# Two-layer transformer on one core: the row shift in two steps, the FFN's chunk stores regrouped, the absorbed weights stored from GpSimd's queue

## The chip, the cores and the metric

The kernel runs on one core of a Trainium2 chip. The metric is device time in microseconds (us) of one execution. The core has engines with instruction streams of their own: TensorE (PE, matrix products and transposes), VectorE (DVE), ScalarE (ACT), GpSimd (POOL) and SyncE (SP), which only issues DMAs here. They are tied together by semaphores: an instruction that waits holds up everything that is written behind it on its engine. Tiles have 128 partitions; PSUM banks take what PE produces, everything else of a core is in SBUF, and large intermediate results go through device memory (`..._dram`).

## The reference

The input x is [2, 1024, 512] in float32. Four residual blocks follow each other:

```python
x = x + layernorm(attn0(layernorm(x), Wq, Wk, Wv, Wo))          # 16 heads, rotary, causal
x = x + layernorm(ffn0(layernorm(x), w_gate, w_up, w_down))      # silu(gate) * up, hidden 2048
x = x + layernorm(attn1(layernorm(x), q_a, q_b, kv_a, kv_b, o))  # latent attention, 16 heads
x = x + layernorm(ffn1(layernorm(x), w_gate_up, w_proj))         # ternary weights, rms norm of the hidden

def layernorm(x, eps=1e-5):
    m = mean(x, -1); v = var(x, -1)
    return (x - m) / sqrt(v + eps)

def ternary_quant(w):          # per 64 weights of a row, in bf16
    scale = clip(mean(abs(w)), 1e-8)
    return clip(round(w / scale), -1, 1) * scale
```

The normalised row is x · rstd + shift, with rstd = 1 / sqrt(v + eps) and shift = −m · rstd. attn1 is computed with absorbed weights: for each head the product of the key expansion with the query weight (`wabs`, 128x384) and of the value expansion with the output weight (`wov`, 128x512), so that keys and values stay latent.

## The kernel before

The 2048 rows of x are 16 tiles of 128 rows. The program is a row of stages; each stage is a block in which every engine has its own written order, and a stage's tiles have a prefix in the profile. The ones that matter here, in order of time:

- `l0o` (`project_residual_norm`, about 632 to 700): output projection of attention 0, layernorm of its result (`which` 0), residual add, layernorm of the sum (`which` 1), transpose. 16 tiles, a software pipeline written by hand. Per tile VectorE takes statistics (L605), aggregates them into mean and variance (L610), inverts the standard deviation that ACT makes (L615), forms the shift (L617), and subtracts for the low half of the transposed tile (L637). GpSimd has two operations a tile, a low half (L650) and the residual add (L657).
- `f0f` (`feed_forward`, layer 0, about 701 to 1287): the hidden dimension in groups; a span of rows at a time. Beside its matmuls the stage quantises the weights of layer 1's FFN, 48 chunks of 128x512. ACT casts a chunk, VectorE and GpSimd compute levels and result, and SyncE stores it into `gate_up_q` or `down_q`. There are two chunk buffers and two result buffers in turn. GpSimd's last step on a chunk (L2072, out `f0f_quant`) waits until the store of two chunks ago has let its buffer go; GpSimd also makes the low halves of the hidden tile (L2056, `f0f_h_hl`), which PE's second product (L1890, `f0f_ybank`) waits for. PE works through the groups in pairs, and 12 chunks fall into one pair (`TURN_CHUNKS`).
- the weights stage (`residual_norm_and_weights`, about 1287 to 1383; tiles `w_`, `wk_`, `f_acc`): residual and norms of f0f's result for 16 tiles (shift: L2346; GpSimd adds the residual, L2385), joined with transposes of layer 1's weights, and then for 16 heads the products `wabs` and `wov`. Each head's two results are copied out of PSUM by ACT (L2325) and VectorE (L2377) into two buffers in turn, and stored. The query weights come in four loads `load_q`, the output weights in four loads `load_ow`.
- `l1p` (`latent_operands`): the latent operands of layer 1's attention, half of the rows at a time. The second one (l1p1, about 2051 to 2141) also does residual and norm of 8 row tiles of the first half (`rows`): statistics (L2573), inverse (L2578), shift (L2580), aggregate of the next tile (L2586) on VectorE, std (L2492) and the row itself (L2497) on ACT, the query's rotation (L2617, 128x1024) and the residual add (L2622) on GpSimd.
- `f1n` (`residual_norm_transposed`, about 2707 to 2751): the same for the input of layer 1's FFN, 16 tiles, some with one and some with two norms, 24 in all (shift: L236).

In each of the four functions the shift is one VectorE operation on 128x1, out of two inputs in SBUF:

```python
dve.wait_ge(std_done[which], t + 1)
nc.vector.reciprocal(rstd[...], std[...])
dve.wait_ge(rstd_done[which], t + 1)
nc.vector.scalar_tensor_tensor(out=shift[...], in0=mv[..., 0:1], scalar=-1.0, in1=rstd[...],
                               op0=ALU.mult, op1=ALU.mult)      # (mean * -1) * rstd
```

The counts are 32 (l0o), 24 (weights stage), 8 (l1p1) and 24 (f1n), 88 in all. SyncE's queue is written out in each stage. In f0f it alternates `load_chunk(c)`, which waits for the cast of chunk c − 2, with `store_chunk(c - 5)`, which waits for that chunk's L2072; at the third of every six chunks it also loads the weights of a coming group (`x_raw`). In the weights stage it ends with the stores of the heads and, between them, the last three weight loads. All DMAs of the program are issued by SyncE.

Of the kernel before, what the change touches and what calls it, by code (L numbers as in the profile page):

```python
# [18 lines left out]
ALU = mybir.AluOpType  # L19
AX = mybir.AxisListType  # L20

P = 128
# [152 lines left out]
def residual_norm_transposed(nc, m, ident, done_rows, acc, src, dst, xT_hl, loads):  # L175
# [8 lines left out]
    std, rstd, shift = (m.sb(n, [P, 2, RING]) for n in ("std", "rstd", "shift"))  # L184
# [6 lines left out]
    stats_done, mv_done, std_done, rstd_done, shift_done = ([m.sem(f"{n}{i}") for i in range(2)] for n in (  # L191
        "stats_done", "mv_done", "std_done", "rstd_done", "shift_done"))
# [12 lines left out]
    with nc.Block() as block:  # L205
# [15 lines left out]
        def _(dve):  # L221
            nc.vector.memset(eps[:, :], EPS_LN).then_inc(eps_set, 1)

# [255 lines left out]
def project_residual_norm(nc, m, ident, tiles, src, dst, oT, raw, xT_hl, loads):  # L479
# [11 lines left out]
    std, rstd, shift = (m.sb(n, [P, 2, RING]) for n in ("std", "rstd", "shift"))  # L491
# [8 lines left out]
    stats_done, mv_done, std_done, rstd_done, shift_done = ([m.sem(f"{n}{i}") for i in range(2)] for n in (  # L500
        "stats_done", "mv_done", "std_done", "rstd_done", "shift_done"))
    with nc.Block() as block:
# [93 lines left out]
        def _(dve):  # L596
            nc.vector.memset(eps[:, :], EPS_LN).then_inc(eps_set, 1)
            for k in range(KT):
# [13 lines left out]
            def inverse(which, t):  # L612
                r = t % RING
                dve.wait_ge(std_done[which], t + 1)
                nc.vector.reciprocal(rstd[:, which, r:r + 1], std[:, which, r:r + 1]).then_inc(rstd_done[which], 1)  # L615
                dve.wait_ge(rstd_done[which], t + 1)
                nc.vector.scalar_tensor_tensor(out=shift[:, which, r:r + 1], in0=mv[:, which, r, 0:1], scalar=-1.0,  # L617
                                               in1=rstd[:, which, r:r + 1], op0=ALU.mult, op1=ALU.mult
                                               ).then_inc(shift_done[which], 1)
# [1022 lines left out]
TURN_CHUNKS = 12  # L1642
NGR = D // GROUP
# [74 lines left out]
def feed_forward(nc, m, ident, xT_hl, acc, gate, up, down, raw, ternary=None, chunks=None, rows=None):  # L1718
# [81 lines left out]
    def _(sp):  # L1800
# [40 lines left out]
        else:  # L1841
            for g in range(2, NG + 2):
                first = (g - 2) * TURN_CHUNKS // 2
                for c in range(first, first + TURN_CHUNKS // 2):
                    load_chunk(c)
                    if c >= 5:
                        store_chunk(c - 5)
                    if g < NG and c == first + 2:
                        load(g, g % 2)
            for c in range(len(chunks) - 5, len(chunks)):  # L1850
                store_chunk(c)
# [251 lines left out]
def residual_norm_and_weights(nc, m, ident, src, dst, acc, w, waT, wpT, xT_hl, loads, wabs_dram, wov_dram):  # L2103
# [8 lines left out]
    std, rstd, shift = (m.sb(n, [P, 2, RING]) for n in ("std", "rstd", "shift"))  # L2112
# [29 lines left out]
    stats_done, mv_done, std_done, rstd_done, shift_done = ([m.sem(f"{n}{i}") for i in range(2)] for n in (  # L2142
        "stats_done", "mv_done", "std_done", "rstd_done", "shift_done"))
# [6 lines left out]
    with nc.Block() as block:  # L2150
        @block.sync
        def _(sp):
# [178 lines left out]
        def _(dve):  # L2331
            nc.vector.memset(eps[:, :], EPS_LN).then_inc(eps_set, 1)

# [7 lines left out]
            def inverse(which, t):  # L2341
                r = t % RING
                dve.wait_ge(std_done[which], t + 1)
                nc.vector.reciprocal(rstd[:, which, r:r + 1], std[:, which, r:r + 1]).then_inc(rstd_done[which], 1)
                dve.wait_ge(rstd_done[which], t + 1)
                nc.vector.scalar_tensor_tensor(out=shift[:, which, r:r + 1], in0=mv[:, which, r, 0:1], scalar=-1.0,  # L2346
                                               in1=rstd[:, which, r:r + 1], op0=ALU.mult, op1=ALU.mult
                                               ).then_inc(shift_done[which], 1)
# [30 lines left out]
        @block.gpsimd  # L2379
        def _(pool):  # L2380
            for t in range(NT):
                g = t // PAIR
                pool.wait_ge(z_done, t + 1)
                pool.wait_ge(x_loaded[g % 2], 16 * (g // 2 + 1))
                nc.gpsimd.tensor_tensor(acc[:, t, :], acc[:, t, :], x[:, g % 2, t % PAIR, :], ALU.add).then_inc(sum_done, 1)  # L2385

def latent_operands(nc, m, ident, xT_hl, waT, wpT, norm_w, rope, out, stores=(), rows=None):
# [29 lines left out]
    if rows is not None:  # L2419
# [3 lines left out]
        r_std, r_inv, r_shift = (m.sb(n, [P, 2]) for n in ("r_std", "r_inv", "r_shift"))  # L2423
        eps_ln = m.sb("eps_ln", [P, 1])
# [3 lines left out]
    with nc.Block() as block:  # L2428
# [368 lines left out]
```

## Time and profile before

| | us |
|---|---|
| median of 3 runs (lowest, highest) | 3134.84 (3132.80, 3139.66) |
| the profiled execution | 3139.53 |
| its span in the trace | 3137.8 |

| engine | busy us | share of the span |
|---|---|---|
| PE | 2870.7 | 91% |
| DVE | 1858.1 | 59% |
| ACT | 1289.9 | 41% |
| POOL | 1058.7 | 34% |

The mean granted clock of TensorE in this execution is 0.952 of full speed. The share of a whole span says little about a change that touches some stages of 40 to 600 us: for those the timeline (each instruction with its start, its duration and, in brackets, the idle time before it and what ended it), the waits by line and windows of 10 us are the views. In a timeline row the duration is from start to end; on VectorE the next instruction can start some hundredths of a us before the end of the one before. SPq stands for SyncE's instructions, which issue DMAs.

### The profile page before, as it was taken

The page shows a single profiled execution, that of the slowest core. Times are in us where ns is not written, and L with a number is a line of the kernel's source. Part 1 is how long each engine was busy: PE and PEld are TensorE (multiplying, and loading weights), DVE is VectorE, ACT ScalarE, POOL GpSimd, SP SyncE. Part 2 cuts the span into 40 slices and gives each one's busy share as a digit, 9 for nine tenths or more (in the row PEclk, how much of TensorE's full clock was granted, in tenths as well). Part 3 has the DMA queues.
Part 4 walks back from the last instruction along what each step waited for, and adds up shares of the span by engine and source line. Part 5 has one row for each costly group of instructions (what it writes and reads, how often), then busy time and mean ns, then how long its engine had stood idle before and what let it go on. Part 6 is the DMA issues. An engine that isn't in the chain of part 4 may idle for free. (4 is left out here: it accounts for less than half of the span.)

```text
span 3137.8 us, 43073 instructions
## 1 busy us (share of the span) xinstructions
PE 2870.7 (91%) x14636; PEld 2292.3 (73%) x14636; DVE 1858.1 (59%) x3604; ACT 1289.9 (41%) x2488; POOL 1058.7 (34%) x844
## 2 busy tenths in 40 slices
PE   7969999879999999687999999786999999699998
PEld 5846666567787878466888888675888888478886
DVE  5647878674454535634566666665666666744446
ACT  2216666562121222432444444333444444543334
POOL 1217777764454536414111111043111111132223
PEclk9979999989999999799999999988999999789999
DMA  4774444142121201560000000121000000200012
GB/s 163 236 224 133 133 121 135 53 155 79 42 64 42 64 22 39 188 258 21 13 18 12 12 18 3 55 91 47 12 12 18 12 12 4 101 21 21 10 37 81
DMA packets 136084, 217.86 MB, mean 69 GB/s; under 512 B 14513, under 2 KB 85169, under 8 KB 135441
## 3 DMA queue, kind: packets, MB, share of 16 engines
q1 hardware_dynamic: 135952, 216.19, 21.5%
q8 instruction: 73, 1.20, 0.2%
q14 instruction: 59, 0.48, 0.0%
HBM read 144.05 MB, written 71.83 MB: 69 GB/s over the span
## 5 line engine op out<-in xcount | busy, mean ns | idle before, releaser
L1246 POOL TENSOR_TENSOR l0a_probs_hl<-l0a_probs,l0a_probs_hl 128x896 fp32r<-128x896 f32 (+1 forms) x128 | 285.2, 2247 | 107.1 <-ACT l0a_probs L1174 107.1
L1511 ACT ACTIVATE l1a_probs<-l1a_scores,l1a_row 128x128 f32<-128x128 f32 (+7 forms) x256 | 189.7, 742 | 320.2 <-DVE l1a_row L1556 320.2
L1566 DVE TENSOR_TENSOR l1a_pT_hl<-l1a_work,l1a_pT_hl 128x512 fp32r<-128x512 f32 (+3 forms) x384 | 213.2, 555 | 171.1 <-ACT l1a_pT_hl L1518 170.9
L1618 POOL TENSOR_TENSOR l1a_wabs<-l1a_wabs_raw,l1a_wabs 128x384 fp32r<-128x384 f32 x32 | 32.5, 1016 | 816.9 <-ACT l1a_wabs L1527 816.9
L1485 PE MATMUL l1a_obank<-l1a_pT_hl,l1k_v_hl 128*128 128x512 f32 (+3 forms) x1152 | 300.7, 370 | 7.1 <-DVE l1a_pT_hl L1566 7.1
L1465 PE MATMUL l1a_scores<-l1k_kT_hl,l1a_qa_hl 128*128 128x512 f32 (+3 forms) x1152 | 291.8, 362 | 1.5 <-ACT l1a_probs L1511 1.5
L1493 PE MATMUL l1a_work<-l1a_wov,l1a_oT_hl 128*128 128x512 f32 x768 | 215.6, 404 | 5.0 <-DVE l1a_oT_hl L1585 3.0
L1518 ACT CAST l1a_pT_hl<-l1a_work 128x512 fp32r<-128x512 f32 (+3 forms) x384 | 183.8, 479 | 84.8 <-PE l1a_work L1476 83.5
L1556 DVE TENSOR_REDUCE l1a_row<-l1a_scores 128x1 f32<-128x128 f32 (+7 forms) x256 | 189.9, 751 | 44.4 <-PE l1a_scores L1468 44.3
L1890 PE MATMUL f0f_ybank<-f0f_wT,f0f_h_hl 128*128 128x512 f32 x768 | 196.7, 406 | 12.6 <-POOL f0f_h_hl L2056 12.5
L1485 PEld LDWEIGHTS l1a_obank<-l1a_pT_hl,l1k_v_hl 128*128 128x128 f32 x1152 | 181.5, 191 | 33.3 <-DVE l1a_pT_hl L1566 14.9
L1580 DVE SCALAR_TENSOR_TENSOR l_acc<-l1a_work,l1a_row,l_acc 128x512 f32<-128x512 f32 x256 | 189.0, 748 | 28.2 <-PE l1a_work L1493 21.3
L1465 PEld LDWEIGHTS l1a_scores<-l1k_kT_hl,l1a_qa_hl 128*128 128x128 f32 x1152 | 188.8, 191 | 21.7 <-ACT l1a_probs L1511 1.8
L1465 PE MATMUL l1a_scores<-l1k_kpe,l1a_q_stack 128*128 128x512 f32 (+3 forms) x768 | 203.4, 346 | 0.0
L1476 PE MATMUL l1a_work<-all_ident,l1a_probs 128*128 128x128 f32 x1152 | 192.3, 276 | 9.6 <-DVE l1a_qa_hl L1571 6.2
L1880 PE MATMUL f0f_gbank<-x_xT,f0f_wT 128*128 128x512 f32 x768 | 192.5, 400 | 1.4 <-DVE f0f_wT L1960 1.4
L1880 PE MATMUL f0f_ubank<-x_xT,f0f_wT 128*128 128x512 f32 x768 | 189.5, 395 | 0.0
L1966 DVE TENSOR_TENSOR f0f_hid<-f0f_silu,f0f_ubank 128x512 f32<-128x512 f32 x64 | 44.0, 688 | 229.9 <-PE f0f_ubank L1880 212.4
L1173 ACT ACTIVATE l0a_probs_hl<-l0a_sbank 128x896 fp32r<-128x896 f32 (+1 forms) x128 | 124.5, 972 | 135.2 <-PE l0a_sbank L1139 78.0
L1890 PEld LDWEIGHTS f0f_ybank<-f0f_wT,f0f_h_hl 128*128 128x128 f32 x768 | 145.1, 194 | 44.6 <-issue 9.3
L1476 PEld LDWEIGHTS l1a_work<-all_ident,l1a_probs 128*128 128x128 f32 x1152 | 140.6, 141 | 48.2 <-DVE l1a_qa_hl L1571 12.9
L2053 POOL TENSOR_TENSOR f1x_squares<-f1x_squares,f1f_sq 128x512 f32<-128x512 f32 x64 | 82.9, 1296 | 269.1 <-ACT f1f_sq L1925 269.1
(272 smaller groups left out, 6398.3 us busy)
## 6 DMA issues: line engine op xcount, KB each, us to landing
v_dram<-l0f_v_rows SPq DMA_DIRECT2D x24, 768.0 KB, 4.2
qk_dram<-l0f_stage SPq DMA_DIRECT2D x128, 128.0 KB, 2.5
l0a_v_stage<-v_dram SPq DMA_DIRECT2D x32, 384.0 KB, 4.2
l0a_q_stack<-qk_dram SPq DMA_DIRECT2D x32, 256.0 KB, 3.5
l0a_k_stack<-qk_dram SPq DMA_DIRECT2D x32, 256.0 KB, 3.8
f0f_chunk<-in_L_ffn_w_gate_up SPq DMA_DIRECT2D x32, 256.0 KB, 2.7
l1a_wov_raw<-wov_dram SPq DMA_DIRECT2D x32, 256.0 KB, 2.7
l0a_v_stage<-v_dram SPq DMA_DIRECT2D x8, 768.0 KB, 6.4
```

Of the source, the lines that this page charges most:

```text
L1246: nc.gpsimd.tensor_tensor(probs_hl[:, r, 1, 0:wide], probs[:, r, 0:wide], f32(probs_hl[:, r, 0, 0:wide]), ALU.subtract).then_inc(low_done, 1)
L1465: last = pe.matmul(scores[:, buf, cols], lhs, rhs, start=(i == 0), stop=(not diagonal and i == len(steps) - 1))
L1476: last = pe.transpose(work[:, slot, i * P:(i + 1) * P], probs[s][:, first + n, :], ident[:, :])
L1485: last = pe.matmul(obank[:, c:SPAN], src["v_hl"][:, a, n, :], pT_hl[:, ring(n, s), b, c:SPAN], start=(n == 0 and i == 0), stop=(n == QT * ...
L1493: last = pe.matmul(work[:, slot, :], oT_hl[:, s, a, n * P:(n + 1) * P], wov[:, hp, b, :], start=(i == 0), stop=(i == 2))
L1511: nc.scalar.activation(probs[s][:, first:first + wide, :].rearrange("p k c -> p (k c)"), scores[:, n % S_AHEAD, 0:wide * P], ACT.Exp, bias ...
L1518: nc.scalar.copy(pT_hl[:, ring(n, s), 0, c:SPAN], work[:, slot, c:SPAN]).then_inc(turned_high, 1)
L1556: nc.vector.tensor_reduce(row[:, 0, row_slot:row_slot + 1], scores[:, n % S_AHEAD, 0:wide * P], AX.X, ALU.max, negate=True).then_inc(max_d ...
L1566: nc.vector.tensor_tensor(pT_hl[:, r, 1, c:SPAN], work[:, slot, c:SPAN], f32(pT_hl[:, r, 0, c:SPAN]), ALU.subtract).then_inc(work_free[slo ...
L1580: nc.vector.scalar_tensor_tensor(out=out[:, t, :], in0=work[:, slot, :], scalar=row[:, 2, row_slot:row_slot + 1], in1=out[:, t, :], op0=AL ...
L1880: last = pe.matmul(bank[:, b, :], wT[:, half, wa, w, c * HG + b * P:c * HG + (b + 1) * P], xT_hl[:, xa, c, a * SPAN:(a + 1) * SPAN], start ...
L1890: last = pe.matmul(ybank[:, b % 2, :], h_hl[:, a % 2, ht, ha, b * P:(b + 1) * P], wT[:, half, wa, 2, ht * D:(ht + 1) * D], start=(n == 0), ...
```

## The change

Three things change.

1. In four functions the shift is made by two tensor_tensor operations: `minus = zero - mean`, which needs the aggregate only and stands ahead of the wait for the standard deviation, and `shift = minus * rstd` behind the reciprocal. A column of zeros is set once per stage.
2. In f0f the stores of chunks are regrouped: with 12 chunks in a group pair, the second of them is followed by four stores (c − 5 to c − 2) and the next three by none; everywhere else a load is followed by the one store as before.
3. In the weights stage the 32 stores of the heads' results are issued by GpSimd on its own queue, behind its 16 row adds. SyncE issues the last three weight loads one after the other.

```diff
 # the four functions with a layernorm (names as in project_residual_norm)
+            nc.vector.memset(zero[:, :], 0.0).then_inc(zero_set, 1)
+            dve.wait_ge(zero_set, 1)
             def inverse(which, t):
                 r = t % RING
+                dve.wait_ge(mv_done[which], t + 1)
+                nc.vector.tensor_tensor(minus[:, which, r:r + 1], zero[:, :], mv[:, which, r, 0:1], ALU.subtract
+                                        ).then_inc(minus_done[which], 1)
                 dve.wait_ge(std_done[which], t + 1)
                 nc.vector.reciprocal(rstd[:, which, r:r + 1], std[:, which, r:r + 1]).then_inc(rstd_done[which], 1)
+                dve.wait_ge(minus_done[which], t + 1)
                 dve.wait_ge(rstd_done[which], t + 1)
-                nc.vector.scalar_tensor_tensor(out=shift[:, which, r:r + 1], in0=mv[:, which, r, 0:1], scalar=-1.0,
-                                               in1=rstd[:, which, r:r + 1], op0=ALU.mult, op1=ALU.mult
-                                               ).then_inc(shift_done[which], 1)
+                nc.vector.tensor_tensor(shift[:, which, r:r + 1], minus[:, which, r:r + 1], rstd[:, which, r:r + 1],
+                                        ALU.mult).then_inc(shift_done[which], 1)
...
 # feed_forward
+QUANT_LAG = 5
+def chunks_to_store(c):
+    behind, place = c - QUANT_LAG, c % TURN_CHUNKS
+    if behind < 0 or 2 <= place < QUANT_LAG:
+        return []
+    return range(behind, c - 1) if place == 1 else [behind]
                 for c in range(first, first + TURN_CHUNKS // 2):
                     load_chunk(c)
-                    if c >= 5:
-                        store_chunk(c - 5)
+                    for done in chunks_to_store(c):
+                        store_chunk(done)
...
 # residual_norm_and_weights, SyncE
-            def store_head(h):
-                sp.wait_ge(a_read, h + 1)
-                sp.dma_start(wabs_dram[h], wabs[:, h % 2]).then_inc(a_stored[h % 2], 16)
-                sp.wait_ge(v_read, h + 1)
-                sp.dma_start(wov_dram[h], wov[:, h % 2]).then_inc(v_stored[h % 2], 16)
-            for h in range(NH):
-                store_head(h)
-                if h == 1:
-                    load_ow(2)
-                if h == 3:
-                    load_q(3)
-                if h == 5:
-                    load_ow(3)
+            load_ow(2)
+            load_q(3)
+            load_ow(3)
 # residual_norm_and_weights, GpSimd, behind the row adds
+            for h in range(NH):
+                pool.wait_ge(a_read, h + 1)
+                pool.dma_start(wabs_dram[h], wabs[:, h % 2]).then_inc(a_stored[h % 2], 16)
+                pool.wait_ge(v_read, h + 1)
+                pool.dma_start(wov_dram[h], wov[:, h % 2]).then_inc(v_stored[h % 2], 16)
```

VectorE in l1p1, one tile, before (`l1p_r_shift` is the shift, `l1p_r_mv` mean and variance, `l1p_r_inv` the inverse):

```order
L2568 TENSOR_TENSOR l1p_crossed<-l1p_pbank,l1x_sin 128x16x32 x2
L2573 BN_STATS l1p_r_stats<-l_acc 128x6
L2578 RECIPROCAL l1p_r_inv<-l1p_r_std 128x1
L2580 SCALAR_TENSOR_TENSOR l1p_r_shift<-l1p_r_mv,l1p_r_inv 128x1
L2586 BN_AGGR l1p_r_mv<-l1p_r_stats 128x2
L2536 TENSOR_TENSOR l1p_k_parts<-l1p_down,l1x_cos 128x64
```

The same place after:

```order
L2595 TENSOR_TENSOR l1p_crossed<-l1p_pbank,l1x_sin 128x16x32 x2
L2600 BN_STATS l1p_r_stats<-l_acc 128x6
L2604 TENSOR_TENSOR l1p_r_minus<-l1p_zero,l1p_r_mv 128x1
L2608 RECIPROCAL l1p_r_inv<-l1p_r_std 128x1
L2611 TENSOR_TENSOR l1p_r_shift<-l1p_r_minus,l1p_r_inv 128x1
L2616 BN_AGGR l1p_r_mv<-l1p_r_stats 128x2
L2563 TENSOR_TENSOR l1p_k_parts<-l1p_down,l1x_cos 128x64
```

Two operations with two SBUF inputs stand around the reciprocal where one stood behind it; the aggregate of the next tile follows both. In l0o it is the same, twice a tile.

SyncE in f0f at the boundary of two group pairs, before (`f0f_chunk` is a load, `gate_up_q` a store, `x_raw` the next weights):

```order
L1808 DMA f0f_chunk<-in_L_ffn_w_gate_up 128x512
L1812 DMA gate_up_q<-f0f_quant 128x512
L1808 DMA f0f_chunk<-in_L_ffn_w_gate_up 128x512
L1812 DMA gate_up_q<-f0f_quant 128x512
L1804 DMA x_raw<-in_L_ffn_w_gate 128x2x512
L1804 DMA x_raw<-in_L_ffn_w_up 128x2x512
L1804 DMA x_raw<-in_L_ffn_w_down 128x4x256
L1808 DMA f0f_chunk<-in_L_ffn_w_gate_up 128x512
L1812 DMA gate_up_q<-f0f_quant 128x512
```

The same place after:

```order
L1831 DMA f0f_chunk<-in_L_ffn_w_gate_up 128x512
L1835 DMA gate_up_q<-f0f_quant 128x512 x4
L1831 DMA f0f_chunk<-in_L_ffn_w_gate_up 128x512
L1827 DMA x_raw<-in_L_ffn_w_gate 128x2x512
L1827 DMA x_raw<-in_L_ffn_w_up 128x2x512
L1827 DMA x_raw<-in_L_ffn_w_down 128x4x256
L1831 DMA f0f_chunk<-in_L_ffn_w_gate_up 128x512 x3
L1835 DMA gate_up_q<-f0f_quant 128x512
```

The first load is that of chunk 13 (25, 37); the stores of chunks 9 to 11 have moved from behind the loads 14 to 16 to ahead of load 14.

SyncE at the heads of the weights stage, before (a pair L2179, L2181 for each head; `w_arena` is `load_ow`, `w_q_nope` is `load_q`):

```order
L2179 DMA wabs_dram<-w_wabs 128x384
L2181 DMA wov_dram<-w_wov 128x512
L2175 DMA w_arena<-in_L_attn_o_w 128x4x512
L2179 DMA wabs_dram<-w_wabs 128x384
L2181 DMA wov_dram<-w_wov 128x512
L2179 DMA wabs_dram<-w_wabs 128x384
L2181 DMA wov_dram<-w_wov 128x512
L2167 DMA w_q_nope<-in_L_attn_q_b_w 128x4x384
```

and GpSimd's stream after, from its row adds on:

```order
L2404 TENSOR_TENSOR f_acc<-f_acc,w_x 128x512 x16
L2407 DMA wabs_dram<-w_wabs 128x384
L2409 DMA wov_dram<-w_wov 128x512
L2407 DMA wabs_dram<-w_wabs 128x384
L2409 DMA wov_dram<-w_wov 128x512
```

All 32 stores stand on GpSimd now, in the order of the heads, with no load between them.

## Rows read from the trace of the kernel before

**Rows 1.** Waits of PE and POOL, 701 to 1287: total us, times, longest

```profile
PE f0f_ybank L1890 <- POOL f0f_h_hl L2056: 12.5, 3, 4.2
...
POOL f0f_quant L2072 <- DMA gate_up_q<-f0f_quant: 24.9, 2, 12.5
```

**Rows 2.** Timeline (start, duration us) of the FFN, SyncE, GpSimd, PE, one boundary

```profile
849.65 0.33 SPq L1808 DMA_DIRECT2D f0f_chunk<-in_L_ffn_w_gate_up  x1
...
850.02 0.43 SPq L1812 DMA_DIRECT2D gate_up_q<-f0f_quant  x1
...
853.02 1.15 POOL L2072 TENSOR_TENSOR f0f_quant<-f0f_wb,f0f_ratio 128x512 bf16<-128x512 bf16 x1 [12.46 <-DMA gate_up_q<-f0f_quant]
...
855.51 5.37 PE L1890 MATMUL f0f_ybank<-f0f_wT,f0f_h_hl 128*128 128x512 f32 x12 [4.23 <-POOL f0f_h_hl L2056]
```

**Rows 3.** Windows; busy us: PE, PEld, DVE, ACT, POOL; granted clock, DMA share, GB/s

```profile
660.00:670.00 10.00, 10.00 (x52) 8.23 (x51) 9.79 (x24) 6.94 (x17) 7.76 (x7) 1.00 0.24 87
...
680.00:690.00 10.00, 6.35 (x35) 4.78 (x33) 9.49 (x33) 8.28 (x18) 4.82 (x5) 1.00 0.27 100
...
1320.00:1330.00 10.00, 7.08 (x30) 5.56 (x29) 9.79 (x29) 9.15 (x20) 4.35 (x4) 0.50 1.02 371
...
1350.00:1360.00 10.00, 8.98 (x48) 5.88 (x48) 2.77 (x4) 3.90 (x10) 0.00 (x0) 1.00 1.00 345
...
2733.00:2747.00 14.00, 9.54 (x36) 5.94 (x34) 13.36 (x45) 12.86 (x27) 0.04 (x1) 0.50 0.05 19
```

**Rows 4.** One line's instructions (l0o, then l1p1): count, then ns minimum/median/maximum

```profile
L617 DVE SCALAR_TENSOR_TENSOR l0o_shift<-l0o_mv,l0o_rstd x32: 159/455/1171, 643.2 to 695.8; 128x1 f32<-128x1 f32 x32
...
L2580 DVE SCALAR_TENSOR_TENSOR l1p_r_shift<-l1p_r_mv,l1p_r_inv x8: 160/1796/2389, 2066.1 to 2132.1; 128x1 f32<-128x1 f32 x8
```

**Rows 5.** Timeline of VectorE and GpSimd: layer 0 attention, then l0o

```profile
231.13 2.09 POOL L1246 TENSOR_TENSOR l0a_probs_hl<-l0a_probs,l0a_probs_hl 128x896 fp32r<-128x896 f32 x1 [23.97 <-ACT l0a_probs L1174]
...
232.97 0.27 DVE L1199 TENSOR_TENSOR l0a_negmax<-l0a_halves 128x4 f32<-128x4 f32 x1
...
660.36 1.29 POOL L657 TENSOR_TENSOR l0o_z<-l0o_z,l0o_x 128x512 f32<-128x512 f32 x1
...
660.54 1.13 DVE L617 SCALAR_TENSOR_TENSOR l0o_shift<-l0o_mv,l0o_rstd 128x1 f32<-128x1 f32 x1
...
661.61 1.29 POOL L650 TENSOR_TENSOR l0o_ot_hl<-l_oT,l0o_ot_hl 128x512 fp32r<-128x512 f32 x1
...
661.84 1.07 DVE L617 SCALAR_TENSOR_TENSOR l0o_shift<-l0o_mv,l0o_rstd 128x1 f32<-128x1 f32 x1
```

**Rows 6.** Timeline of GpSimd, VectorE and ACT in l1p1, one tile

```profile
2083.74 2.39 POOL L2617 TENSOR_TENSOR l1k_qpe<-l1p_direct,l1p_crossed 128x1024 f32<-128x1024 f32 x1 [2.17 <-DVE l1p_crossed L2568]
...
2084.35 1.79 DVE L2580 SCALAR_TENSOR_TENSOR l1p_r_shift<-l1p_r_mv,l1p_r_inv 128x1 f32<-128x1 f32 x1
...
2086.07 0.17 DVE L2586 BATCH_NORM_AGGREGATE l1p_r_mv<-l1p_r_stats 128x2 f32<-128x6 f32 x1
...
2086.09 1.30 POOL L2622 TENSOR_TENSOR l_acc<-l_acc,l1p_x 128x512 f32<-128x512 f32 x1
...
2086.27 0.29 ACT L2492 ACTIVATE l1p_r_std<-l1p_r_mv,l1p_eps_ln 128x1 f32<-128x1 f32 x1 [6.03 <-DVE l1p_r_mv L2586]
...
2094.30 1.80 DVE L2580 SCALAR_TENSOR_TENSOR l1p_r_shift<-l1p_r_mv,l1p_r_inv 128x1 f32<-128x1 f32 x1
```

**Rows 7.** Timeline of SyncE's queue in the weights stage: first two and last

```profile
1343.19 0.34 SPq L2179 DMA_DIRECT2D wabs_dram<-w_wabs  x1
...
1345.16 0.33 SPq L2179 DMA_DIRECT2D wabs_dram<-w_wabs  x1
...
1379.98 0.33 SPq L2181 DMA_DIRECT2D wov_dram<-w_wov  x1
```

**Rows 8.** Waits in the weights stage, 1287 to 1383

```profile
DVE w_wov L2377 <- DMA wov_dram<-w_wov: 22.1, 12, 4.6
...
ACT w_wabs L2325 <- DMA wabs_dram<-w_wabs: 15.9, 9, 4.3
```

More of the change, by code:

```diff
@@ L183, in residual_norm_transposed @@
     stats, mv = m.sb("stats", [P, 2, RING, 6]), m.sb("mv", [P, 2, RING, 2])
-    std, rstd, shift = (m.sb(n, [P, 2, RING]) for n in ("std", "rstd", "shift"))
+    std, rstd, minus, shift = (m.sb(n, [P, 2, RING]) for n in ("std", "rstd", "minus", "shift"))
+    zero = m.sb("zero", [P, 1])
     eps = m.sb("eps", [P, 1])
@@ L490, in project_residual_norm @@
     stats, mv = m.sb("stats", [P, 2, RING, 6]), m.sb("mv", [P, 2, RING, 2])
-    std, rstd, shift = (m.sb(n, [P, 2, RING]) for n in ("std", "rstd", "shift"))
+    std, rstd, minus, shift = (m.sb(n, [P, 2, RING]) for n in ("std", "rstd", "minus", "shift"))
+    zero = m.sb("zero", [P, 1])
     eps = m.sb("eps", [P, 1])
@@ L613, in inverse @@
                 r = t % RING
+                dve.wait_ge(mv_done[which], t + 1)
+                nc.vector.tensor_tensor(minus[:, which, r:r + 1], zero[:, :], mv[:, which, r, 0:1], ALU.subtract
+                                        ).then_inc(minus_done[which], 1)
                 dve.wait_ge(std_done[which], t + 1)
                 nc.vector.reciprocal(rstd[:, which, r:r + 1], std[:, which, r:r + 1]).then_inc(rstd_done[which], 1)
+                dve.wait_ge(minus_done[which], t + 1)
                 dve.wait_ge(rstd_done[which], t + 1)
-                nc.vector.scalar_tensor_tensor(out=shift[:, which, r:r + 1], in0=mv[:, which, r, 0:1], scalar=-1.0,
-                                               in1=rstd[:, which, r:r + 1], op0=ALU.mult, op1=ALU.mult
-                                               ).then_inc(shift_done[which], 1)
+                nc.vector.tensor_tensor(shift[:, which, r:r + 1], minus[:, which, r:r + 1], rstd[:, which, r:r + 1],
+                                        ALU.mult).then_inc(shift_done[which], 1)
             for i in range(tiles + 9):
@@ L1845, in _ @@
                     load_chunk(c)
[L1846 to L1847 removed]
+                    for done in chunks_to_store(c):
+                        store_chunk(done)
                     if g < NG and c == first + 2:
                         load(g, g % 2)
[L1850 removed]
+            for c in range(len(chunks) - QUANT_LAG, len(chunks)):
                 store_chunk(c)
@@ L2111, in residual_norm_and_weights @@
     stats, mv = m.sb("stats", [P, 2, RING, 6]), m.sb("mv", [P, 2, RING, 2])
-    std, rstd, shift = (m.sb(n, [P, 2, RING]) for n in ("std", "rstd", "shift"))
+    std, rstd, minus, shift = (m.sb(n, [P, 2, RING]) for n in ("std", "rstd", "minus", "shift"))
+    zero = m.sb("zero", [P, 1])
     eps = m.sb("eps", [P, 1])
@@ L2342, in inverse @@
                 r = t % RING
+                dve.wait_ge(mv_done[which], t + 1)
+                nc.vector.tensor_tensor(minus[:, which, r:r + 1], zero[:, :], mv[:, which, r, 0:1], ALU.subtract
+                                        ).then_inc(minus_done[which], 1)
                 dve.wait_ge(std_done[which], t + 1)
                 nc.vector.reciprocal(rstd[:, which, r:r + 1], std[:, which, r:r + 1]).then_inc(rstd_done[which], 1)
+                dve.wait_ge(minus_done[which], t + 1)
                 dve.wait_ge(rstd_done[which], t + 1)
-                nc.vector.scalar_tensor_tensor(out=shift[:, which, r:r + 1], in0=mv[:, which, r, 0:1], scalar=-1.0,
-                                               in1=rstd[:, which, r:r + 1], op0=ALU.mult, op1=ALU.mult
-                                               ).then_inc(shift_done[which], 1)
+                nc.vector.tensor_tensor(shift[:, which, r:r + 1], minus[:, which, r:r + 1], rstd[:, which, r:r + 1],
+                                        ALU.mult).then_inc(shift_done[which], 1)
             for i, j in joined_steps(J):
@@ L2575, in _ @@
                     t = i - 1
+                    dve.wait_ge(r_mv_done, t + 1)
+                    nc.vector.tensor_tensor(r_minus[:, t % 2:t % 2 + 1], zero[:, :], r_mv[:, t % 3, 0:1], ALU.subtract
+                                            ).then_inc(r_minus_done, 1)
                     dve.wait_ge(r_std_done, t + 1)
```

34 lines of the change are left out of this document (23 added, 11 removed).

## The prediction

> **What bounds the kernel now.** I read the waits of the FFN stage of layer 0 first, then the timeline at the longest of them, then the row-norm stages by line, by timeline and by windows, and last the stage that makes the absorbed weights. TensorE is the long engine of nearly every stage, so an edit counts only where PE waits, or where a short stage is held by another engine. The three parts of the change meet three such places.
>
> In the FFN of layer 0 PE waits three times for GpSimd's low halves of the hidden tile, 12.5 us together [rows 1]. The timeline gives the chain once in full [rows 2]: SyncE issues the load of chunk 14 at 849.65 and, behind it in program order, the store of chunk 9 at 850.02; GpSimd's last step on chunk 11 (L2072), which writes over chunk 9's buffer (two buffers in turn), starts at 853.02 after 12.46 us of waiting for that store; its low halves (L2056) come behind, and PE starts 4.23 us late. The store had been ready long before; it stood behind a load that was waiting.
>
> In the projection stage of layer 0 (l0o) PE and VectorE are both full between 660 and 670, and from 680 on VectorE alone (9.49 of 10 us, PE 6.35) [rows 3]. The second half of f1n and the middle of the weights stage are VectorE's too (13.36 of 14, 9.79 of 10 us) [rows 3].
>
> The rows that compute the shift are what to look at there [rows 4]: an operation on 128x1 takes 0.16 us at the least, but its median is 0.455 us in l0o and 1.796 in l1p1. The timeline says why [rows 5]: the shift of 660.54 ends (661.67) when GpSimd's L657 ends (661.65), and the one of 661.84 ends (662.91) with GpSimd's L650 (662.90). A VectorE operation with two inputs in SBUF waits for the GpSimd operation then running. A plain tensor_tensor does the same: L1199 at 232.97 ends at 233.24, GpSimd's operation at 233.22, and it took 0.27 [rows 5].
>
> In the weights stage the 16 DMA engines are full (share 1.00 at 1350 to 1360) [rows 3], and the head loop's stores run from 1343.19 to 1379.98 [rows 7]. ACT and VectorE wait there 15.9 and 22.1 us for earlier stores to let go of their buffers [rows 8].
>
> **Part 1, chunk stores: a gain of 12.5 us.** At each pair boundary four stores are issued behind load 13, none behind loads 14 to 16. SyncE now waits for GpSimd's chunk 11 ahead of load 14, whose own release did not come before 849.65 [rows 2]; GpSimd was free for chunk 11 at 853.02 − 12.46 = 840.56 and needs about 1.15 us for it, so the stores are out by about 842 and the new wait is covered by 7 us. If it weren't, load 14 and the loads of the next weights behind it would be late. Without the stall L2072 starts at 840.56, L2056 follows its own input, and PE's 4.23 us are gone. Nothing else waits there: the three waits are all that PE has for L2056 [rows 1]. Bounds: 0, if another wait ends at the same moment, to −12.5. I take −12.5, since L2072 is late by 12 us and PE by 4.
>
> **Part 2, row shifts.** One operation becomes two, both with two SBUF inputs, 88 times. minus moves ahead of the reciprocal, so it takes over the wait that the shift had; the question is whether the shift then waits a second time. Where GpSimd runs two operations back to back it does: 660.36 and 661.61 follow each other, and two shifts 1.3 us apart both waited [rows 5].
> - l1p1 (8 tiles): GpSimd's L2617 runs from 2083.74 to 2086.13 and L2622 starts at 2086.09, for 1.30 [rows 6]. The shift of 2084.35 waits for the first and ends at 2086.14. In the changed kernel minus ends there, the reciprocal follows, and the shift falls into L2622, to about 2087.39; the aggregate, which started at 2086.07, starts some 1.27 later. Behind it hang ACT's std (2086.27, idle for 6.03 before and waiting for just this) and then the whole tile [rows 6]. The first tile's shift meets no GpSimd operation and the last one's wait is followed by idle time, so six tiles: 6 × 1.27 = 7.6 us. Bounds: 8 × 0.16 = 1.3 without a second wait, 8 × 1.3 = 10.4.
> - l0o (32 shifts): 32 × 0.16 = 5.1 if no added operation waits, 32 × 0.455 = 14.6 at the median of the present ones. Of the two shifts of a tile mostly one meets GpSimd, so half and half, 16 × 0.455 + 16 × 0.16 = 9.8, less the first tiles, where VectorE still has room: 9.
> - f1n (24): GpSimd is idle in the stretch that VectorE holds, so only those in it, some nine, lie on the path at 0.16 each: 1.5. Bounds 0.5 and 3.8 (all 24).
> - Weights stage rows (24): I take ten for VectorE's full stretch, 1.5; the rest lies under loads. Bounds 0 and 3.8.
>
> The four memsets run once per stage and are nothing.
>
> **Part 3, stores on GpSimd's queue.** SyncE loses 32 issues of 0.34 us [rows 7] and issues the loads of ow(2), q(3) and ow(3) as soon as their buffers are free; GpSimd, which has nothing else to do after its 16 adds, gets the 32. No DMA issued by GpSimd is in this trace, so the price of an issue is open. From below, SyncE's 0.34; from above and nearest, since it is the same engine on a 128x512 tile, its 1.29 us operation [rows 5]. The 32 stores span 36.79 us now, 1.187 apart. At 1.29 they span 31 × 1.29 = 40.0, +3.2 us at the end of the stage, whose last store the next stage waits for. At 0.34 GpSimd holds nothing up; the first stores of the two first heads are 1.97 apart [rows 7], so they could span 15 × 1.97 = 29.6 and one store more, some 6 us less than now. The full DMA engines forbid most of that, because the same bytes have to pass and stores that overtake loads delay what PE needs. I take +3.2; each 0.1 us more per issue adds 3.1.
>
> The Trainium skill ("DMA: Bandwidth & Descriptors", "Issuing engines are not separate DMA queues") says that DMAs started by different engines run on the same 16 DMA engines, and that another issuing engine saves only the time of issuing. Going by that page part 3 would be worth 0, and the sum 3.2 us less. No run so far shows GpSimd's queue here.
>
> **Sum:** −12.5 + 7.6 + 9 + 1.5 + 1.5 + 3.2 = +10.3 us. The profiled execution took 3139.53 us (span 3137.8), so it would take 3149.8. It lies 4.7 above the median of the runs, 3134.84; on that median the forecast is 3145.
>
> **Rivals.**
> - GpSimd issues slowly. An issue longer than any 128x512 operation, say 1.6 us, makes part 3 31 × (1.6 − 1.187) = 12.8 instead of 3.2: 3155. For it: no row sets an upper bound on this price. Against: SyncE's 0.34. It decides from 1.19 us on.
> - The other side, faster: the shift slips in. If minus only takes over the wait, and the reciprocal and the shift run before GpSimd's next operation has begun, part 2 costs its unblocked price (l1p1 1.3, l0o 5.1, f1n 0.5, weights 0.5: 7.4), and the stores, no longer behind loads, gain part of their 6 us, say 4: −12.5 + 7.4 − 4 = −9, 3126; with part 3 at 0, 3130. The point it turns on is whether GpSimd's next operation has started when the reciprocal is done. For it: the aggregate at 2086.07 was not held. Against: L2622 had started at 2086.09 and 661.84 waited behind 660.54 all the same; and the aggregate has one input.
> - Part 3 is worth nothing, only the issuing engine differs: −12.5 + 7.6 + 9 + 1.5 + 1.5 = +7.1, 3142. For it: the DMA engines are full whoever issues, so the bytes set the end. This is what the page above would make of it. Against: the stores no longer keep their place among the loads.
> - Part 1 does not do what it says: PE's wait moves to another cause and 8 or more of the 12.5 us stay. +18 to +23, 3153 to 3158. Against: one releaser is named for all three.
> - The clock: longer holes in l1p1 and l0o let the granted clock, 0.50 in f1n and the weights stage and 1.00 in l0o's full stretch [rows 3], fall in stages that now have it at 1.00. Half speed over a tile or two adds 5 to 10: 3150 to 3155.
>
> **How the numbers follow.** Forecast (3137 to 3153) 0.45, slow issue 0.14, slipping in 0.22, part 3 nothing 0.07, part 1 nothing 0.05, clock 0.07. A measurement of this kernel tells 0.2% (6.3 us) from no change, so faster is below 3128.6 and slower above 3141.1. Of the forecast 0.10 falls within, of slipping in 0.10, of the third rival 0.05: same 0.25. Faster is what is left of slipping in, 0.12. The rest, 0.63, is slower. The range goes from 3128 to 3158: 0.12 lie below, about 0.05 above. The likeliest case alone has 3137 to 3153.
>
> **What will show it.** In the changed profile L2072 has no wait for the stores and PE none for L2056 over 3 us. In l1p1 the new shift takes about 1.1 us beside L2622 and the tiles stand 11.2 us apart instead of 9.95; if they still stand 9.95 apart, the shift slipped in. In l0o the blocked time of both new lines exceeds that of L617 now, and the stage ends about 9 us later. The last store on GpSimd's queue, less the first, is 40 us by the forecast, under 37 if issuing is cheap, 49 if slow. The prediction is wrong if the second wait is missing, or if GpSimd's issue is far from 1.29 us.

## The result, and the profile after

The changed kernel takes 3144.19 us (median of 8 runs, 3140.34 to 3147.92) beside 3135.37 us of the kernel before on the same chip. The ratio is 1.0025, 95% interval 1.0015 to 1.0036: slower by 5 to 11 us. The profiled execution has a span of 3144.9 us at a mean granted clock of 0.952.

Part 1 of the page after (engine, busy us, share of the span, instructions):

```profile
PE 2868.1 (91%) x14636; PEld 2290.7 (73%) x14636; DVE 1879.3 (60%) x3696; ACT 1289.4 (41%) x2488; POOL 1075.4 (34%) x876
```

VectorE is busy 21 us longer (1858.1 before), PE 2.6 us less, at the same mean granted clock as before. The sums over the whole span don't show which stage gained and which lost. To see that, I took for each stage the time from its first matmul to the first of the next stage, out of the lines of TensorE's tiles in each trace (us):

| stage | before | after | part 1 alone | part 2 alone | part 3 alone |
|---|---|---|---|---|---|
| l0o | 73.5 | 84.0 | 73.5 | 83.9 | 75.4 |
| f0f | 586.4 | 566.8 | 566.9 | 586.3 | 586.7 |
| weights stage | 86.9 | 90.5 | 87.3 | 87.9 | 91.3 |
| l1p1 | 97.7 | 105.8 | 98.8 | 105.9 | 98.5 |
| l1a1 (attention, second half) | 568.5 | 572.5 | 566.3 | 572.6 | 566.0 |
| f1n | 38.0 | 39.3 | 37.8 | 39.3 | 37.9 |

After less before, the six make +10.5 − 19.6 + 3.6 + 8.1 + 4.0 + 1.3 = +7.9; the other stages add −0.8, which gives the 7.1 between the two spans. Stages that no kernel here changes differ by over 4 us between profiles (l1a0: 567.6 to 572.1), so a single us of such a row says nothing. (l1a0 and l1a1 are the two halves of layer 1's attention.)

**The FFN.** The waits of PE in f0f after the change, against [rows 1]:

```profile
PE f0f_wbank L1894 <- DVEq L1970: 3.4, 1, 3.4
PE f0f_gbank L1903 <- DVE f0f_wT L1983: 1.4, 1, 1.4
PE f0f_wbank L1894 <- DVE f0f_wT L1983: 1.1, 2, 0.5
```

No wait for GpSimd's low halves is left. SyncE's timeline at the boundary, against [rows 2]: the last two of the four stores, then load 14.

```profile
845.90 9.15 SPq L1835 DMA_DIRECT2D gate_up_q<-f0f_quant  x2
862.52 0.34 SPq L1831 DMA_DIRECT2D f0f_chunk<-in_L_ffn_w_gate_up  x1
```

The second of these two stores waited (9.15 us for both) and went out at 855; load 14 follows at 862.52, when its own wait ended. The cover of 7 us is there. But the stage is 19.6 us shorter, and the waits were only 12.5. Windows of the kernel before at the three stalls, with the granted clock third from the end, and one of part 1 alone at the first of these places:

```profile
850.00:860.00 10.00, 5.77 (x17) 4.23 (x16) 1.38 (x2) 0.62 (x1) 3.60 (x3) 0.69 0.62 197
1000.00:1010.00 10.00, 8.48 (x25) 6.73 (x26) 1.38 (x2) 0.00 (x0) 2.62 (x3) 0.66 0.34 113
1140.00:1150.00 10.00, 5.95 (x22) 4.44 (x21) 0.69 (x1) 1.72 (x3) 3.60 (x3) 0.87 0.12 39
```

```profile
842.00:862.00 20.00, 20.00 (x90) 16.20 (x89) 6.80 (x10) 4.56 (x8) 3.38 (x3) 1.00 0.33 112
```

Before, the clock stood at 0.69, 0.66 and 0.87 in the windows of the stalls; without them it stays at 1.00, 2.4 GHz. TensorE's L1890 took 196.7 us in all before (its line of the page) and 190.2 in part 1 alone: 6.5 us of the missing 7.

**l1p1.** Timeline of one tile after, GpSimd, VectorE and ACT, against [rows 6]:

```profile
2079.85 2.39 POOL L2647 TENSOR_TENSOR l1k_qpe<-l1p_direct,l1p_crossed 128x1024 f32<-128x1024 f32 x1 [2.18 <-DVE l1p_crossed L2595]
2082.20 1.29 POOL L2652 TENSOR_TENSOR l_acc<-l_acc,l1p_x 128x512 f32<-128x512 f32 x1
```

```profile
2080.29 1.97 DVE L2604 TENSOR_TENSOR l1p_r_minus<-l1p_zero,l1p_r_mv 128x1 f32<-128x1 f32 x1
...
2082.43 1.07 DVE L2611 TENSOR_TENSOR l1p_r_shift<-l1p_r_minus,l1p_r_inv 128x1 f32<-128x1 f32 x1
2083.43 0.17 DVE L2616 BATCH_NORM_AGGREGATE l1p_r_mv<-l1p_r_stats 128x2 f32<-128x6 f32 x1
...
2091.48 1.97 DVE L2604 TENSOR_TENSOR l1p_r_minus<-l1p_zero,l1p_r_mv 128x1 f32<-128x1 f32 x1
```

```profile
2083.63 0.29 ACT L2517 ACTIVATE l1p_r_std<-l1p_r_mv,l1p_eps_ln 128x1 f32<-128x1 f32 x1 [7.28 <-DVE l1p_r_mv L2616]
```

minus waits for the first GpSimd operation (ends 2082.26, GpSimd's 2082.24), the product falls into the second and ends with it (2083.50, 2083.49); the aggregate and ACT's std stand behind. From minus to minus a tile now takes 11.19 us, against 9.95.

**l0o.** All shifts of l0o before, then the two new lines after (busy us, mean ns):

```profile
L617 DVE SCALAR_TENSOR_TENSOR l0o_shift<-l0o_mv,l0o_rstd 128x1 f32<-128x1 f32 x32 | 17.6, 551 | 1.1
```

```profile
L632 DVE TENSOR_TENSOR l0o_shift<-l0o_minus,l0o_rstd 128x1 f32<-128x1 f32 x32 | 16.5, 517 | 3.3
L626 DVE TENSOR_TENSOR l0o_minus<-l0o_zero,l0o_mv 128x1 f32<-128x1 f32 x32 | 12.7, 396 | 0.0
```

29.2 us instead of 17.6: 11.6 more, 10.5 of which reach the end of the stage.

**The weights stage.** GpSimd's first two and last issue (timeline), against SyncE's 0.34 in [rows 7]:

```profile
1337.26 0.72 POOL L2407 DMA_DIRECT2D wabs_dram<-w_wabs  x1 [5.51 <-ACT w_wabs L2339]
1339.13 0.55 POOL L2409 DMA_DIRECT2D wov_dram<-w_wov  x1 [1.15 <-DVE w_wov L2396]
...
1375.11 0.54 POOL L2409 DMA_DIRECT2D wov_dram<-w_wov  x1 [0.74 <-DVE w_wov L2396]
```

An issue on GpSimd takes 0.54 us, the first 0.72, not 1.29, and GpSimd waits between them for ACT and VectorE (1.15 us here). The 32 stores span 37.85 us, where 36.79 was the span before and 40.0 the forecast.

### The profile page after: what moved, and what is told of

The parts are those of the page before. It is cut to its first block and busy times, and to the rows that moved or that the text cites. A ratio compares the mean times of both kernels' runs of the same rounds, so it can differ in the third digit from the quotient of the medians.

```text
span 3144.9 us, 43255 instructions
## 1 busy us (share of the span) xinstructions
PE 2868.1 (91%) x14636; PEld 2290.7 (73%) x14636; DVE 1879.3 (60%) x3696; ACT 1289.4 (41%) x2488; POOL 1075.4 (34%) x876
## 3 DMA queue, kind: packets, MB, share of 16 engines
q1 hardware_dynamic: 131344, 208.85, 20.9%
## 5 line engine op out<-in xcount | busy, mean ns | idle before, releaser
L1913 PE MATMUL f0f_ybank<-f0f_wT,f0f_h_hl 128*128 128x512 f32 x768 | 190.1, 396 | 0.1
L1903 PEld LDWEIGHTS f0f_gbank<-x_xT,f0f_wT 128*128 128x128 f32 x768 | 145.7, 190 | 36.9 <-DVE f0f_wT L1983 1.8
```

What stands on the lines that cost most here:

```text
L1903: last = pe.matmul(bank[:, b, :], wT[:, half, wa, w, c * HG + b * P:c * HG + (b + 1) * P], xT_hl[:, xa, c, a * SPAN:(a + 1) * SPAN], start ...
L1913: last = pe.matmul(ybank[:, b % 2, :], h_hl[:, a % 2, ht, ha, b * P:(b + 1) * P], wT[:, half, wa, 2, ht * D:(ht + 1) * D], start=(n == 0), ...
```

## The experiments

Each stands against the kernel before, on the same chip; ratios are given with their 95% intervals. The diffs are shortened: semaphore counts, the same edit in other functions and some surrounding lines are left out, and `...` and `[...]` mark gaps.

**e1, part 1 alone**

```diff
                     load_chunk(c)
-                    if c >= 5:
-                        store_chunk(c - 5)
+                    for done in chunks_to_store(c):
+                        store_chunk(done)
```

> Part 1 alone: the regrouped chunk stores of the FFN, everything else as before. By the prediction's step only the three waits of PE go, 12.5 us: 3122 against 3135. The rival read from the changed trace: behind each of these waits TensorE also ran at a lower granted clock (0.69, 0.66 and 0.87 in the 10 us windows around them), and this goes too; the stage would be some 19.7 us shorter: 3115. If the stores do nothing by themselves: 3135.

Measured: 3113.80 us, ratio 0.9928 (0.9915 to 0.9941), 19 to 27 us faster. f0f takes 566.9 us instead of 586.4. The larger number holds; that the wait alone goes (3122) is out.

**e2, part 2 alone**

```diff
+                nc.vector.tensor_tensor(minus[:, which, r:r + 1], zero[:, :], mv[:, which, r, 0:1], ALU.subtract)
...
-                nc.vector.scalar_tensor_tensor(out=shift[...], in0=mv[..., 0:1], scalar=-1.0, in1=rstd[...], ...)
+                nc.vector.tensor_tensor(shift[...], minus[...], rstd[...], ALU.mult)
```

> Part 2 alone: the shift as minus and product in the four functions, the stores all as before. Theory, the second wait: l1p1 +6.5 (the new shift takes 1.07 us beside GpSimd's residual add), l0o +10, weights stage +2, f1n +1.3, together +20: 3155. Rival, minus only takes over the wait: +7.4, 3142.

Measured: 3162.45 us, ratio 1.0082 (1.0069 to 1.0095), 22 to 30 us slower. l0o +10.4, weights stage +1.0, l1p1 +8.2, f1n +1.3, together 20.9; l1a1 is 4.1 longer too, which none of my terms had and of which more below. The second wait is there, slipping in is out.

**e3, part 3 alone**

```diff
-            for h in range(NH):
-                store_head(h)          # SyncE, with the three loads between the heads
+            load_ow(2)
+            load_q(3)
+            load_ow(3)
...
+            for h in range(NH):        # GpSimd, behind its row adds
+                pool.wait_ge(a_read, h + 1)
+                pool.dma_start(wabs_dram[h], wabs[:, h % 2]).then_inc(a_stored[h % 2], 16)
+                pool.wait_ge(v_read, h + 1)
+                pool.dma_start(wov_dram[h], wov[:, h % 2]).then_inc(v_stored[h % 2], 16)
```

> Part 3 alone: the 32 stores on GpSimd's queue, SyncE with the three loads. The changed trace shows 0.54 us for an issue on GpSimd, far under 1.29, so the forecast's mechanism (GpSimd as the bound) should be absent. If the stage's end is set by the bytes: 0, 3135. If the order of the transfers or the landing of the last store on this queue costs, as the two traces side by side suggest: +2 to +4, 3137 to 3139. If the prediction's own step held: +3.2 with the stores 1.29 apart.

Measured: 3140.43 us, ratio 1.0009 (0.9998 to 1.0020): between nothing and 6 us slower. The weights stage takes 91.3 us against 86.9. In its timeline PE waits for VectorE's copies of `wov`, and these wait for stores:

```profile
1356.31 1.10 PE L2265 MATMUL w_vbank<-w_owT,w_v_b 128*128 128x512 f32 x2 [3.03 <-DVE w_wov L2366]
...
1367.26 1.10 PE L2265 MATMUL w_vbank<-w_owT,w_v_b 128*128 128x512 f32 x2 [4.13 <-DVE w_wov L2366]
```

```profile
DVE w_wov L2366 <- DMA wov_dram<-w_wov: 21.2, 9, 6.6
```

In all VectorE waits no longer for its stores than before (22.1 us) [rows 8]; it is the longest of these waits that grew, from 4.6 to 6.6 us.

From issue to landing of the `wov` stores (the tile's view), before and then in e3:

```profile
DMA to landing us min/median/max: 2.0/4.0/5.8
```

```profile
DMA to landing us min/median/max: 2.2/2.4/8.3
```

Most stores land sooner beside the loads than behind them (median 2.4 us against 4.0), but the slowest takes 8.3 instead of 5.8, and each result has two buffers only.

**e4, part 1, and the shift as one operation with one tensor input**

```diff
-                nc.vector.scalar_tensor_tensor(out=shift[:, which, r:r + 1], in0=mv[:, which, r, 0:1], scalar=-1.0,
-                                               in1=rstd[:, which, r:r + 1], op0=ALU.mult, op1=ALU.mult)
+                nc.vector.tensor_scalar(shift[:, which, r:r + 1], mv[:, which, r, 0:1], rstd[:, which, r:r + 1], -1.0,
+                                        ALU.mult, ALU.mult)
```

> Part 1, and the shift as one operation with one tensor input: mean times the column rstd (as the scalar operand) times -1; stores of the heads on SyncE as before. Theory A, it is the second tensor input from SBUF that makes VectorE wait for GpSimd's running operation: all 88 shifts take about 0.16 us, l1p1 loses 1.6 us on six tiles (-10), l0o up to -12, f1n and the weights stage -1 to -4 together, on top of part 1: 3090 to 3100. Theory B, any operation that reads two columns from SBUF waits, the scalar operand too: no gain over part 1 alone, 3115.

Measured: 3098.25 us, ratio 0.9876 (0.9859 to 0.9892), the fastest version here, 34 to 44 us ahead of the kernel before and about 15 ahead of part 1 alone. The shift no longer waits (line groups with busy us and mean ns):

```profile
L616 DVE TENSOR_SCALAR l0o_shift<-l0o_mv,l0o_rstd 128x1 f32<-128x1 f32 x32 | 6.8, 214 | 1.1
...
L2586 DVE TENSOR_SCALAR l1p_r_shift<-l1p_r_mv,l1p_r_inv 128x1 f32<-128x1 f32 x8 | 1.7, 214 | 0.3
```

0.214 us each time, where they had 0.551 on average in l0o (above) and 1.662 in l1p1 before:

```profile
L2580 DVE SCALAR_TENSOR_TENSOR l1p_r_shift<-l1p_r_mv,l1p_r_inv 128x1 f32<-128x1 f32 x8 | 13.3, 1662 | 0.3
```

l1p1 falls to 89.1 us and f1n to 34.3; but l0o only to 71.9. Of the 12 us for l0o in my expectation 1.6 came, no more than l0o differs between profiles in which it is unchanged (73.5 to 75.4). PE is as full there as it was, with VectorE at 8.16 of 10 us instead of 9.51 (window of e4, then of the kernel before):

```profile
670.00:680.00 10.00, 10.00 (x52) 8.24 (x51) 8.16 (x29) 8.55 (x19) 8.04 (x7) 1.00 0.42 161
```

```profile
670.00:680.00 10.00, 9.95 (x50) 8.08 (x49) 9.51 (x30) 9.84 (x22) 7.60 (x7) 1.00 0.55 182
```

So taking VectorE's waits away uncovers PE, while 10.5 of the 11.6 us added to VectorE reached the end.

**e5, part 3 with the loads held at their old place among the heads**

```diff
+            sp.wait_ge(v_read, 2)
             load_ow(2)
+            sp.wait_ge(v_read, 4)
             load_q(3)
+            sp.wait_ge(v_read, 6)
             load_ow(3)
```

> Part 3 alone, but SyncE holds each of the three weight loads until the results of heads 2, 4 and 6 have been read out, the place in the order of heads where they stood before. In the run of part 3 alone the head loop (first to last transpose of output weights) took 38.2 us against 33.5, with two waits of PE for VectorE's w_wov of 3.0 and 4.1 us. If the order of the loads among the stores costs that: the head loop is back at 33 to 35, 3136. If the stores being on GpSimd's queue costs it: 37 to 39 as before this edit, 3139 to 3140.

Measured: 3143.92 us, ratio 1.0026 (1.0016 to 1.0035). The head loop takes 40.8 us, the whole stage 94.6, in a profile of the longest of its ten executions (3148.59 us). That the loads overtake the stores is not what costs: held back, it is no better, and by this profile worse.

**e6, the counterpart: stores on SyncE, the three loads on GpSimd**

```diff
-                if h == 1:
-                    load_ow(2)         # and load_q(3), load_ow(3), on SyncE
...
+            load_ow(2)                 # on GpSimd, behind its row adds
+            load_q(3)
+            load_ow(3)
```

> The counterpart: the stores of the heads stay on SyncE, and GpSimd issues the three weight loads behind its row adds, each with its own wait only, so the loads no longer stand among the stores but on the other queue. If what costs is that loads and stores run on two queues without an order between them: head loop 37 to 39, 3139. If it is the stores on GpSimd's queue: 33 to 35, 3136 or below.

Measured: 3138.09 us, ratio 1.0011 (0.9998 to 1.0024). The head loop takes 36.2 us, between the two expectations. It could not have told them apart: in e1 and e8, where nothing in this stage is changed, the loop takes 37.4 and 36.4 us. The whole stage is steadier (86.9 to 87.4 in the three kernels that leave it as it was). Here it takes 84.9 us, no longer than with everything on SyncE, although its slowest `wov` store takes 8.0 us too. Read by the stage of this one profile, two queues without an order between them show no cost; read by the median nothing is decided.

**e7, part 2 with minus made from one input**

```diff
-                nc.vector.tensor_tensor(minus[:, which, r:r + 1], zero[:, :], mv[:, which, r, 0:1], ALU.subtract)
+                nc.vector.tensor_scalar(minus[:, which, r:r + 1], mv[:, which, r, 0:1], -1.0, None, ALU.mult)
```

> Part 2 alone with minus made from one input (mean times -1 by a constant) instead of zero minus mean; the product still has two inputs, and there are still 176 operations. Theory, the cost is the second wait: minus never waits and the product waits where the old shift did; l1p1 back from 105.9 to about 98, l0o from 83.9 to 74 to 76, sum +2 to +5 over before, 3138 to 3141. Rival, the cost is one more operation and its semaphore on VectorE: near the 3162 of part 2 alone.

Measured: 3141.68 us, ratio 1.0016 (1.0006 to 1.0026): 20 us of part 2's 26 are gone, with the same number of operations. Its l1p1 lines:

```profile
L2617 DVE TENSOR_TENSOR l1p_r_shift<-l1p_r_minus,l1p_r_inv 128x1 f32<-128x1 f32 x8 | 12.4, 1544 | 0.8
...
L2610 DVE TENSOR_SCALAR l1p_r_minus<-l1p_r_mv 128x1 f32<-128x1 f32 x8 | 1.1, 135 | 0.0
```

minus takes 0.135 us and never waits; the product waits as the old shift did (1.544 against 1.662). In the changed kernel minus had waited:

```profile
L2604 DVE TENSOR_TENSOR l1p_r_minus<-l1p_zero,l1p_r_mv 128x1 f32<-128x1 f32 x8 | 12.0, 1505 | 0.0
```

l1p1 is back at 97.8 and l0o at 76.0. The cost of part 2 is the second wait; the operation itself and its semaphores leave +2 to +8 us in all.

**e8, the stall left in, TensorE kept busy through it**

```diff
                 elif kind == "D":
+                    if ternary is None and b == 0 and (half, a) == (1, SPANS - 1) and at < len(events) - QT:
+                        pe.wait_ge(y_read, seen["D"] + 1)
+                        for _ in range(10):
+                            pe.matmul(ybank[:, b % 2, :], wT[:, half, 0, 2, 0:P], xT_hl[:, 0, 0, 0:SPAN],
+                                      start=True, stop=True)
                     if b == 0:
                         pe.wait_ge(h_low, seen["K"] + HT)
```

> The kernel before, with its stall in the FFN left in, but TensorE kept busy through it: ten matmuls whose result is overwritten stand ahead of the wait for the low halves, three times (some 3.9 us of work each in a wait of 4.2). Theory, part 1 gained 12.5 us of waiting and some 7 us of granted clock lost behind the waits: with the clock kept, the stage is about 6 to 7 us shorter although the wait stays, 3129. Rival, the gain beyond 12.5 came from elsewhere (transfers, GpSimd): no change, 3135, or a little slower where the matmuls outlast the wait.

Measured: 3131.10 us, ratio 0.9985 (0.9975 to 0.9994): 30 useless matmuls make the kernel 2 to 8 us faster. f0f takes 580.6 us, 5.8 less. The timeline at the first stall, then the windows of the first and the third:

```profile
851.66 2.49 PE L1889 MATMUL f0f_ybank<-x_xT,f0f_wT 128*128 128x512 f32 x10
856.00 3.00 PE L1896 MATMUL f0f_ybank<-f0f_wT,f0f_h_hl 128*128 128x512 f32 x12 [1.84 <-POOL f0f_h_hl L2062]
```

```profile
850.00:860.00 10.00, 8.16 (x35) 6.30 (x34) 2.06 (x3) 0.79 (x2) 3.62 (x3) 1.00 0.64 197
...
1140.00:1150.00 10.00, 8.18 (x29) 6.20 (x28) 1.38 (x2) 0.21 (x1) 3.62 (x3) 0.83 0.00 0
```

The ten matmuls took 2.49 us, not 3.9, so 1.84 us of idle time are left, but the granted clock is 1.00 where it was 0.69. At the second stall it stays at 1.00 too; at the third, with as much idle time left (1.82 us), it falls as before. The 5.8 us come from the first two. The low clock behind a stall is a cost of its own.

**e9, the stores on ACT's queue**

```diff
             for h in range(NH):        # ACT
                 ...                    # its two copies
+                act.wait_ge(a_read, h + 1)
+                act.dma_start(wabs_dram[h], wabs[:, h % 2]).then_inc(a_stored[h % 2], 16)
+                if h >= 1:
+                    act.wait_ge(v_read, h)
+                    act.dma_start(wov_dram[h - 1], wov[:, (h - 1) % 2]).then_inc(v_stored[(h - 1) % 2], 16)
```

> Part 3 with the 32 stores on ACT's queue in place of GpSimd's, behind ACT's own copies, the wov store of a head one head later; SyncE with the three loads. From the first load of the stage to the next stage the runs with stores on SyncE took 83 to 88 us, those with stores on GpSimd 90 to 95. If it is GpSimd's queue that costs: 84 to 88, 3133 to 3137. If stores that run beside the loads on any second queue cost it: 90 and more, 3139 and more; ACT's 32 issues of about 0.33 us may add some.

Measured: 3138.50 us, ratio 1.0013 (1.0003 to 1.0023), stage 87.9 us. That is the upper end of the runs with stores on SyncE (83.1 to 87.9) and below all with stores on GpSimd (90.5, 91.3, 94.6), each of them one profile; the median says slower by 1 to 7 us. It leans to GpSimd's queue as the dearer one and doesn't exclude that any second queue costs something.

## Why the prediction was right, and where it was not

The forecast was 3145, the median is 3144.19, and the direction came out. But it is right in part by chance: the term of part 1 was 7 us too small, and in the profiles a loss of 4 us that I had not seen, with 1.3 us more on the shifts, made up for most of it.

- **Part 1, −12.5: the term was too small; it measured −19.6 in f0f** (e1: 566.9 against 586.4). The step that failed is "PE's 4.23 us are gone": it priced the stall by the idle time alone. Behind each of the three stalls TensorE ran below full clock; e8, which kept the clock up behind two of them and left the stalls in, shows these two to be worth some 6 us. I had the clock among the rivals, but only as a loss that longer holes could bring, never as one that a removed hole gives back.
- **l1p1, +7.6: measured +8.1.** minus waits for the rotation, the product for the residual add, and the tile period went from 9.95 to 11.19, against 11.2 forecast.
- **l0o, +9: measured +10.5.** Half and half was about right: mean 0.396 and 0.517 us for the two lines.
- **f1n +1.5 and rows of the weights stage +1.5: measured +1.3 and +1.0** (e2). The second is barely outside what that stage shows unchanged (86.9 to 87.4 us, 87.9 in e2).
- **Part 3, +3.2: the number stood, its reason fell.** GpSimd's issue takes 0.54 us, under the 1.19 from which it would bound the loop. What stretches the stage all the same (3.6 with the rows' 1.0 in it, 4.4 in e3) stays open. Slow stores beside loads are there in e3, but in e6 too, whose stage is not longer; e5 rules out the loads' early place; e6 and e9 lean to GpSimd's queue and don't settle it. The sign that I had named, 40 us from first to last store, did not come (37.85), and it can't decide: the 32 stores span 38.7 us in e1, where they are untouched, and 40.1 in e3, with 0.54 us an issue. The prediction called itself wrong if GpSimd's issue was far from 1.29 us, and by that sign its part 3 was wrong.
- **Not in the sum: l1a1, +4.0.** It is +4.1 in e2 (572.6 us); the nine other profiles have 566.0 to 569.2. Windows of 10 us in the same place of this stage, after and then before:

```profile
2181.00:2191.00 10.00, 8.01 (x38) 7.11 (x37) 4.41 (x10) 4.56 (x12) 4.41 (x4) 0.67 0.11 29
```

```profile
2179.00:2189.00 10.00, 8.00 (x53) 6.87 (x52) 6.13 (x13) 5.36 (x13) 4.57 (x4) 1.00 0.16 46
```

The granted clock stands at 0.67 there against 1.00, with PE busy for 8 us of the 10 in both. Nothing in l1a1 was changed; the stage only begins after a longer l1p1. But the clock also falls at the same place of the first half, l1a0, and there in the kernel before and not in the changed one (before, then after):

```profile
1495.00:1505.00 10.00, 8.00 (x38) 6.92 (x37) 4.46 (x11) 4.52 (x12) 3.71 (x4) 0.70 0.05 8
```

```profile
1491.00:1501.00 10.00, 8.00 (x52) 6.70 (x51) 5.30 (x12) 5.33 (x15) 3.62 (x4) 1.00 0.03 3
```

l1a0 is 2.7 us shorter after (569.4 against 572.1), which stands among the other stages' −0.8. PE is idle for 2.0 us at this place in both halves of all eleven profiles, and the clock falls behind it in six of these 22 (e7 has 0.76 in l1a0, e4 0.83 in l1a1). So the 4 us belong to this pair of profiles; that the longer l1p1 brings them, or that they come in every execution, is not shown.

With the terms measured in the profiles the sum is −19.6 + 8.1 + 10.5 + 1.3 + 1.0 + 2.6 + 4.0 = +7.9 us, and the medians differ by 8.8.

Of the rivals, e2 and e7 rule out the shift that slips in; 0.54 us rules out slow issue; part 1 does what it says. "Part 3 is worth nothing" comes near for the median of e3 (0 to +6), not for the stage. The Trainium skill's rule of the prediction ("DMA: Bandwidth & Descriptors", "Issuing engines are not separate DMA queues") holds in that no time was gained by the second queue in e3, e5 or e9; that it costs nothing is not what e5 and e9 show.

The rule behind part 2 stands in the Trainium skill too ("SBUF — State Buffer", "SBUF: two separate sides"): GpSimd and a VectorE operation with two inputs in SBUF hold a pair of ports in turn, each for a whole instruction. e4 and e7 agree as to the waiting, and add, for 128x1, which inputs count: two tensors wait (1.505 us for minus), a tensor with a column as scalar operand does not (0.214).

## What to carry to other kernels

Where VectorE and GpSimd work side by side, count the VectorE operations with two tensor inputs in SBUF before their length: on 128x1 they cost 0.16 us alone and up to 2.4 us beside GpSimd, and splitting one into two can make it wait twice (1.97 and 1.07 us in a tile of l1p1 instead of 1.79). A column given as scalar operand avoids it (e4). And price a stall of TensorE by its idle time plus the low clock that follows, here half as much again.

## What had not been expected of the hardware

Three idle times of 4.2 us cost 6.5 us more through the granted clock (0.69, 0.66 and 0.87 in the windows around them), and 7.5 us of useless matmuls in them were worth 5.8 us, although the clock still fell behind the third. An issue of a 256 KB store by GpSimd takes 0.54 us beside 0.33 on SyncE. A stage that nothing was changed in (l1a1) took 4 us more in the profiles of two kernels, with 0.67 of the full clock in a window of 10 us; behind the same 2 us of idle time it stayed at 1.00 in most others.
